# Normalising the softmax on GpSimd one step further down the pipeline, and silu then gelu back to back on ScalarE

## The reference

```python
x = x + tanh(g_xattn) * attention(layernorm(x), ctx, itok)   # 16 heads, latent keys and values of width 64
x = x + tanh(g_ffn)   * ffn(layernorm(x))

# attention, per head: (scores are scaled; keys outside itok-8 .. itok are masked)
scores = (q_nope @ k_nope.T + rope(q_rope) @ rope(k_rope).T) * scale
attn   = softmax(where(good, scores, -1e30))
out    = (attn @ v) @ W_o

# ffn
h = silu(bitlinear158(x, w1, b1)); h = gelu(h, approximate=False); h = layer_norm(h, g, b)
return bitlinear158(h, w2, b2)
# bitlinear158(x, w, b): xq = round(x_rms * 127/amax) / (127/amax), ternary w, einsum + b
```

## Time and profile before

| | us |
|---|---|
| median of 3 runs | 267.58 (265.24 to 270.92) |
| the profiled execution | 266.58 |
| its span, first to last instruction | 264.8 |
| up to the first softmax maximum | 43.3 |
| tiles 0 to 2, to the mark of tile 2 | 55.7 |
| from there to the mark of tile 3 | 24.1 |
| the next four tiles, mark to mark | 23.8, 23.6, 23.6, 23.3 |
| from the mark of tile 7 to the end | 47.3 |

### The profile page before, as it was taken

How to read it: one execution, slowest core, us unless ns; L and a number is a source line. 1 busy time by engine, 2 the same in 40 slices (tenths; PEclk the granted TensorE clock), 3 DMA queues, 4 the chain that set the end, 5 groups by cost and what they waited for, 6 DMA issues and landing times.

```text
span 264.8 us, 5090 instructions
## 1 busy us (share of the span) xinstructions
PE 221.6 (84%) x1637; PEld 196.9 (74%) x1644; DVE 204.2 (77%) x510; ACT 147.4 (56%) x327; POOL 85.4 (32%) x126
## 2 busy tenths in 40 slices
PE   1899992989999999799999999999999977934354
PEld 1677981879899899698898898889898966712232
DVE  2694543468969667998999999899989987989871
ACT  2366603634644539554945775495567549859131
POOL 1325441223423323434344333445333340111210
PEclk9999996899999999999999999999999999985557
DMA  6999990000000000000000000000000000000000
GB/s 210 265 217 236 348 375 17 0 0 2 0 2 0 0 4 1 2 1 0 4 20 0 0 19 1 0 0 20 0 0 0 22 0 0 20 0 2 21 20 28
DMA packets 11349, 12.31 MB, mean 46 GB/s; under 512 B 3936, under 2 KB 10336, under 8 KB 11104
## 3 DMA queue, kind: packets, MB, share of 16 engines
q1 hardware_dynamic: 10432, 11.44, 15.3%
q10 hardware_dynamic: 896, 0.61, 0.8%
HBM read 11.00 MB, written 1.05 MB: 45 GB/s over the span
## 4 chain that ended last, share of the span: by engine, by line
DVE 32%; PE 24%; issue 15%; SPq 11%; POOL 6%; DMA 4%; ACT 3%; DVEq 2%; POOLq 0%
SPq L344 11%; DVE qcat L1107 4%; PE bank_ff L891 4%; DMA b_bc<-in_L_ffn_b 4%; POOL h_small L430 3%; PE bank_pair L771 3%; PE bank_lat L872 3%; DVE h L1197 3%; DVE neg_max L1256 3%; DVE turned L1111 3%; PE bank_ff L920 2%; DVE z L1176 2%; DVE h L1166 2%; PE bank_prob L861 2%; DVE lat L1267 2%
## 5 line engine op out<-in xcount | busy, mean ns | idle before, releaser
L404 POOL TENSOR_TENSOR qcat<-qcat,turned 64x256 f32<-64x256 f32 x32 | 23.0, 720 | 106.5 <-DVE turned L1111 106.5
L623 ACT ACTIVATE prob_room<-bank_score,neg_max 128x128 f32<-128x128 f32 x128 | 36.5, 371 | 28.8 <-DVE neg_max L1256 28.5
L872 PE MATMUL bank_lat<-kvc,probT_room 128*128 128x65 f32 (+1 forms) x256 | 32.8, 271 | 3.5 <-ACT probT_room L613 3.5
L849 PEld LDWEIGHTS bank_score<-kcat,qcat 128*128 128x128 f32 x256 | 33.6, 192 | 2.3
L872 PEld LDWEIGHTS bank_lat<-kvc,probT_room 128*128 128x128 f32 x256 | 31.3, 193 | 5.0 <-ACT probT_room L613 5.0
L771 PE MATMUL bank_pair<-qcT,wcat 96*128 96x128 f32 (+1 forms) x256 | 34.8, 280 | 0.0
L849 PE MATMUL bank_score<-kcat,qcat 128*128 128x128 f32 (+1 forms) x256 | 33.7, 275 | 0.0
L1107 DVE TENSOR_TENSOR qcat<-bank_pair,cst 128x512 f32<-128x512 f32 x32 | 21.9, 684 | 14.0 <-PE bank_swap L774 14.0
L771 PEld LDWEIGHTS bank_pair<-qcT,wcat 96*128 96x128 f32 x256 | 32.0, 196 | 0.2 <-DVE wcat L1096 0.2
L604 ACT COPY latT<-bank_lat 128x256 f32<-128x256 f32 x32 | 11.8, 369 | 35.3 <-PE bank_lat L879 35.3
L406 POOL TENSOR_TENSOR qcat<-qcat,turned 64x256 f32<-64x256 f32 x32 | 30.5, 953 | 2.5
(11 more groups left out here) (162 smaller groups left out, 420.8 us busy)
## 6 DMA issues: line engine op xcount, KB each, us to landing
wo<-in_L_xattn_W_o SPq DMA_DIRECT2D x1, 2048.0 KB, 19.2
w_sb<-in_L_ffn_w SPq DMA_DIRECT2D x2, 1024.0 KB, 10.2
out_x<-y SPq DMA_DIRECT2D x8, 128.0 KB, 1.7
wuq<-in_L_xattn_W_uq SPq DMA_DIRECT2D x1, 768.0 KB, 10.9
ctx_all<-in_ctx ACTq DMA_DIRECT2D x2, 256.0 KB, 5.1
x_all<-in_x SPq DMA_DIRECT2D x2, 256.0 KB, 4.8
cst<-in_consts SPq DMA_DIRECT2D x1, 512.0 KB, 7.0
x_all<-in_x SPq DMA_DIRECT2D x1, 512.0 KB, 8.1
```

What stands on the lines that cost most here:

```text
L623: last = nc.scalar.activation(prob[:, k % 2, j, 0:kts * P], src[:, j, :], ACT.Exp, bias=neg_max[:, k % 2, j:j + 1])
L849: last = nc.tensor.matmul(bank[:, j * kts * P:(j + 1) * kts * P], qcat[:, k, hh // 2, hh % 2, :], kcat[:, b, hh % 2, 0:kts * P], start=Fal ...
L872: last = nc.tensor.matmul(bank_lat[:, j * (KVC + 1):(j + 1) * (KVC + 1)], probT[:, k % 2, kt, j, :], kvc1[:, b * KT + kt, :], start=(kt == ...
```

## The change

Five things change at once.

1. The softmax sum comes from the accumulator of the exponentials (`accum_out=esum`). DVE `invert_sums` takes its reciprocal one step later, POOL multiplies the 128 x 512 exponentials by it in SBUF, and the transposes wait for that. `values` now produces the latents already turned (64 rows x 256 columns, two matmuls), so `transpose_lat` and DVE's multiply are gone. With 128 keys everything from `transpose_probs` on runs two steps behind the scores (`turn_lag`), with four buffers of exponentials, and the last quarter of `attn_out` moves to step 2 of the next tile.
2. ACT applies Silu and then Gelu in step 2; its tanh and DVE's product are gone.
3. Of the small operations of `quantise` DVE keeps two. POOL computes the lower bound (power one half, times 1e-5/127), the reciprocal root and the dequantisation factor; for x also the variance terms.
4. DVE waits for b1, b2, g and lb only where it first uses each.
5. All loops are written out.

```diff
@@ SBUF, order of steps
+        def turn_lag(kts):
+            return 2 if kts == 1 else 1
@@ POOL
+            def floor_and_root(small_of, floor_ready):
+                link(small(small_of(FLOOR), small_of(MS), pos_half, ALU.pow))
+                nc.gpsimd.tensor_scalar(small_of(FLOOR), small_of(FLOOR), 1e-5 / QMAX, 1.0, ALU.mult, ALU.mult).then_inc(floor_ready, 1)
+                link(small(small_of(RRMS), small_of(MS), neg_half, ALU.pow))
             def root_hq(c):
                 pool.wait_ge(h_sumsq, c + 1)
                 link(small(hs(MS), hs(SQ), eps1, ALU.add))
-                small(hs(RRMS), hs(MS), pow_half, ALU.pow).then_inc(h_rrms, 1)
+                floor_and_root(hs, h_floor)
+            def dequantise(small_of, layer, deq, scale_ready, count, deq_ready):
+                pool.wait_ge(scale_ready, count)
+                nc.gpsimd.tensor_scalar(deq, small_of(YMAX), small_of(RRMS), wmean[:, layer:layer + 1],
+                                        ALU.mult, ALU.mult).then_inc(deq_ready, 1)
+            def normalise(f, k, kts):
+                n = step_no(f, k)
+                pool.wait_ge(rsum_done, n + 1)
+                p = prob_of(n, kts)
+                nc.gpsimd.tensor_tensor(p, p, rsum[:, k % 2, :].unsqueeze(2).broadcast_to([P, GROUP, kts * P]),
+                                        ALU.mult).then_inc(prob_scaled, 1)
                 for k in range(STEPS):
+                    if step_no(f, k) >= 1:
+                        normalise(*behind(f, k, 1), kts)
                     if step_no(f, k) + AHEAD < N:
                         add_rope_step(*ahead(f, k))
                     feed_forward(f, k)
@@ ACT
                 for j in range(GROUP):
-                    last = nc.scalar.activation(prob[:, k % 2, j, 0:kts * P], src[:, j, :], ACT.Exp,
-                                                bias=neg_max[:, k % 2, j:j + 1])
+                    last = nc.scalar.activation(prob_of(n, kts)[:, j, :], src[:, j, :], ACT.Exp,
+                                                bias=neg_max[:, k % 2, j:j + 1], accum_out=esum[:, k % 2, j:j + 1])
-                        if k == 1 and there(f, 2):
-                            tanh(f - 2)
                         if k == 2 and there(f, 3):
                             copy_h(f - 3, 0)
                         if k == 2 and there(f, 2):
-                            gelu(f - 2)
+                            silu(f - 2)
+                            gelu(f - 2, 1.0)
@@ PE
             def transpose_probs(f, k, kts):
-                pe.wait_ge(exp_done, n + 1)
+                pe.wait_ge(prob_scaled, n + 1)
             def values(f, k, kts):
-                for j in range(GROUP):
-                    for kt in range(kts):
-                        last = nc.tensor.matmul(bank_lat[:, j * (KVC + 1):(j + 1) * (KVC + 1)], probT[:, k % 2, kt, j, :],
-                                                kvc1[:, b * KT + kt, :], start=(kt == 0), stop=(kt == kts - 1))
+                for kt in range(kts):
+                    for o in range(2):
+                        last = nc.tensor.matmul(bank_lat[o * KVC:(o + 1) * KVC, 0:2 * P].rearrange("p (j s) -> p j s", j=2),
+                                                kvc1[:, b * KT + kt, :], probT[:, k % 2, kt, o::2, :],
+                                                start=(kt == 0), stop=(kt == kts - 1))
-            def transpose_lat(f, k): ...
+                if k == 2 and there(f, 1) and lag == 2:
+                    attn_out(f - 1, range(STEPS - 1, STEPS))
@@ DVE
-                link(nc.vector.tensor_scalar(small(YMAX), small(AMAX), small(RRMS), 1e-5, ALU.mult, ALU.max))
-                nc.vector.tensor_scalar(deq, small(YMAX), 1.0 / QMAX, wmean[:, layer:layer + 1], ALU.mult, ALU.mult)
-                link(nc.vector.reciprocal(small(YINV), small(YMAX)))
-                link(nc.vector.tensor_scalar(small(QMUL), small(YINV), QMAX, small(RRMS), ALU.mult, ALU.mult))
+                dve.wait_ge(floor, count)
+                dve.wait_ge(dve_link, amax)
+                nc.vector.tensor_scalar(small(YMAX), small(AMAX), 1.0 / QMAX, small(FLOOR), ALU.mult, ALU.max).then_inc(scale, 1)
+                dve.wait_ge(scale, count)
+                link(nc.vector.reciprocal(small(QMUL), small(YMAX)))
-                    quantise_h(f - 3, lambda: silu(f - 2))
+                    quantise_h(f - 3)
-            def normalise(f, k): ...
+            def invert_sums(f, k):
+                dve.wait_ge(exp_done, n + 1)
+                nc.vector.reciprocal(rsum[:, k % 2, :], esum[:, k % 2, :]).then_inc(rsum_done, 1)
             dve.wait_ge(gates_done, 1)
-            for name in ("b1", "b2", "g", "lb"):
-                dve.wait_ge(in_sems[name], 16)
...
```

More of the change, by code:

```diff
@@ L283, in choose, with run_tiles @@
                 main(KT)
-        LEAD = 3
-        def run_tiles(eng, body, after, before=lambda f: None):
-            for f in range(LEAD):
-                before(f)
+        def run_tiles(body, after):
+            for f in range(F):
                 body(f)
-            before(None)
-            with eng.Fori(LEAD, F - 1) as f:
-                before(f)
-                body(f)
-            before(F - 1)
-            body(F - 1)
             after()
         def slot(c):
-            return 1 if known(c) and c == F - 2 else 0
+            return 1 if c == F - 2 else 0
         def last_tile(c):
-            return known(c) and c == F - 1
+            return c == F - 1
         def down_bank(c):
@@ L379, in _ @@
         def _(pool):
-            half = R // 2
+            rope = R // 2
             pool.wait_ge(consts_made, 1)
@@ L407, in add_rope @@
                 pool.wait_ge(pair_done, s + 1)
-            with pool.Fori(0, B // 2) as i:
-                for e in range(2):
-                    b = 2 * i + e
-                    add_rope(kcat[KVC:P, b, 0, :], kcat[0:R, b, 1, :], turned[KVC:P, e, :], turned[0:R, e, :], b)
+            for b in range(B):
+                add_rope(kcat[KVC:P, b, 0, :], kcat[0:R, b, 1, :], turned[KVC:P, b % 2, :], turned[0:R, b % 2, :], b)
             def add_rope_step(f, k):
@@ L608, in copy_probT @@
                 n = step_no(f, k)
-                if not (known(n) and n < 2):
+                if n >= 2:
                     act.wait_ge(lat_ready, n - 1)
@@ L836, in scores @@
                 lag = 1 if kts == 1 else 0
-                if not (known(n) and n <= lag):
+                if n > lag:
                     pe.wait_ge(exp_done, n - lag)
@@ L905, in up @@
                 pe.wait_ge(xqT_copied, c + 1)
-                if waits and not (known(c) and c < 2):
+                if waits and c >= 2:
                     pe.wait_ge(y_done, c - 1)
@@ L947, in main @@
             def main(kts):
+                lag = turn_lag(kts)
                 def body(f):
@@ L962, in body @@
                             transpose_x(f - 2)
-                        feed_forward_mid(f, k)
-                        if not known(f) or 1 <= n < N + 1:
-                            values(*behind(f, k, 1), kts)
-                        feed_forward_end(f, k)
+                        feed_forward_mid(f, k, lag)
+                        if n >= lag:
+                            values(*behind(f, k, lag), kts)
+                        feed_forward_end(f, k, lag)
                         prepare_end(f, k)
@@ L1237, in feed_forward @@
                 if k == 1 and there(f, 3):
-                    quantise_h(f - 3, lambda: silu(f - 2))
-                elif k == 1 and there(f, 2):
-                    silu(f - 2)
+                    quantise_h(f - 3)
                 if k == 2 and there(f, 1):
@@ L1314, in after @@
                     output(F - 1)
-                run_tiles(dve, body, after, before)
+                run_tiles(body, after)
             choose(dve, main)
```

257 lines of the change are left out of this document (125 added, 132 removed).

## The result

| | before | after |
|---|---|---|
| median of the comparison (20 runs each) | 269.98 | 265.71 |
| lowest to highest | 265.24 to 271.35 | 263.02 to 269.85 |
| the profiled execution, its span | 266.58, 264.8 | 263.1, 261.3 |
| first softmax maximum | 43.32 | 37.39 |
| from there to the mark of tile 2 | 55.74 | 47.91 |

The ratio is 0.989 [0.985, 0.994]: 1.1% faster, which is less than the 2% that count as a change. The forecast was 262.2 us and -2.0%.

The account below looks back on a forecast made before the run. PE and DVE were taken as nearly full, PE alone binding early tiles. From the profiled 266.58 us, -5.2 - 1.9 - 7.9 - 1.7 + 1.2 + 6.0 + 2.3 + 2.8 = -4.4 gave 262.2, range 251 to 271.

Parts of the forecast that it names:

- start, wait: Start: without DVE's four weight waits the first softmax maximum comes at 38.15 instead of 43.32, -5.2 us.
- start clock and tiles 0 to 2: Start and PE-bound first tiles: no clock fall, -1.9 us; no latent transposes and shorter `values`, -7.9 us.
- mark 2 to 3: Move from tile 2 to 3: no `down` and a smaller pause, 22.4 instead of 24.1, -1.7 us.
- four full tiles at full clock: Full tiles: period 23.95 against 23.6, +0.3 us per tile, +1.2 over four.
- falls of the clock in them: Full tiles: PE's pause drops the clock in three of four, 2.0 us lost each, +6.
- tail: From mark 7: later exponentials, multiply and lag less quantisation savings, +2.3 us; clock fall after PE's pause, +2.8 (0 to 5).
- the pause: Full tile, step 3: PE idles 3.4 us ahead of `values`, waiting for ACT's copy of the turned exponentials.
- The slow multiply: Rival, POOL in full tiles: big multiply near 3.2 us, delaying the root twice; 281 us, slower; chance 0.07.
- The early gain: Rival, start and tiles 0 to 2: gain eaten, PE's cut not the bound, weight loads hold start; 268 us; chance 0.13.
- the 84 that was asked: Sign: mark of tile 2 near 84; above 88 would show the forecast wrong.
- The clock did hold: Rival, full tiles: PE's pause does not cost the clock; 253.5 to 256.5 us; chance 0.27.
- Better still: Rival, full tiles: not held by ACT, DVE's 4 us a tile show; period 22, 248 us; chance 0.08.

Follow-up runs that it names:

- 5: Changed kernel, last step of tile 7: DVE's last reciprocal moved ahead of output and moments, 267.6 us; also POOL's last multiply ahead of tile 5's root, 265.6 us.
- 7: Changed kernel with ACT tanh, DVE product and both last-step queues reordered (248.1 us), plus quantise's small operations back on DVE except reciprocal roots: 249.1 us.
- before_waits: Kernel before, with only DVE's waits moved: b1 to its first use, b2, g and lb to the end of tile 2; 261.0 us, ratio 0.986.
- 1: Changed kernel with ACT computing tanh in step 1 and DVE the silu product again, Gelu alone in step 2: 251.5 us, ratio 0.935.
- 2: Changed kernel with tanh and DVE product restored, plus one unread single-column Silu (a table load) ahead of Gelu in step 2: 265.5 us.
- 9: Kernel before with DVE's waits moved, loops written out, and Silu then Gelu on ACT in step 2: 275.5 us, ratio 1.033.

## Why the prediction was wrong, and what of it held

| step | forecast | profiled run |
|---|---|---|
| start, wait | -5.2 | -5.9 |
| start clock and tiles 0 to 2 | -9.8 | -7.8 |
| mark 2 to 3 | -1.7 | -1.4 |
| four full tiles at full clock | +1.2 | +1.1 |
| falls of the clock in them | +6.0 | +1.6 |
| tail | +5.1 | +8.9 |
| sum | -4.4 | -3.5 |

That the sums lie only 0.9 apart is luck: the tail is 3.8 and the first tiles 2.0 dearer than forecast, the falls 4.4 and the start 0.7 cheaper. The forecast gave 0.55 to a gain of more than 2%, and the gain is 1.1% by the ratio.

- *The step that failed is the tail.* It says that "the big multiply and the lag add 0.4, three quantisations give back 0.4 each". This took the last multiply nearly for free, and no line asked what stands ahead of the reciprocal on DVE and of the multiply on POOL. The kernel before had these two lines:

```profile
224.89 1.14 ACT L623 ACTIVATE prob_room<-bank_score,neg_max 128x128 f32<-128x128 f32 x4
232.56 0.48 DVE L1212 SCALAR_TENSOR_TENSOR x_all<-bank_ff,tgate,x_all 128x256 f32<-128x256 f32 x1 [0.31 <-PE bank_ff L891]
```

  Up to the end of these exponentials the changed tail is 3.2 longer (S + 11.7, before S + 8.5), exactly as forecast. From there to the last residual it is 5.7 longer, where 0.4 and 2.8 for the clock were forecast; 2.6 of it are the two queues (5), and the remaining 3.1 agree with the 3.2 of multiply and clock, but no run splits them. From the last residual to the end it takes 32.3, before 32.2, so the 1.2 that the quantisations were to give back did not come. DVE has less to do there but waits for POOL's bound, 0.81 in the first of them (231.80), where it did not wait before, and 1.12 in the second (245.70), where it waited 0.83. Undoing change 3 lengthened the tail by 0.4 in all (7). The 2.6 and the 1.2 are the 3.8 that the forecast lacks.
- *Clock.* The place and the cause were right: PE idle behind ACT's copy. Three falls were forecast at 2.0 each, and the profiled run had one, of 1.6. Their number is not fixed: the profiled runs of 5, whose full tiles are the same, had three, for 5.8 us. The other runs of the changed kernel left no trace; by their mean clocks many had more falls than the profiled one.
- *The time itself.* The forecast was added to the profiled execution of the kernel before, 266.58, as if every run were like it. In the comparison that kernel's median is 269.98, 3.4 above that execution, and the changed kernel's median is 2.6 above its own. So the measured 265.71 lies 3.5 above the forecast though the sums differ by 0.9.
- *Start.* The -5.9 is partly luck too. The changed kernel and the eleven made from it share their code up to the first softmax maximum, and it came at 37.39 in this run, the earliest, and at 37.84 to 40.09 in the others.
- *Tiles 0 to 2* came 2.0 short. In before_waits the clock at the start gave 1.1 and not 1.9. And `values` takes 0.58 from its start to that of the next piece and not 0.47, measured as the 0.84 of the earlier trace rows was, which is 0.11 in each of twelve steps:

```profile
60.52 0.58 PE bank_lat L906 x4
```

- *The full tile* was right leg by leg: the pause is 3.12 for 3.4, the multiply 1.04 for 1.3, DVE's wait 1.84 for 2, the period 23.86 for 23.95. The reason is shown (1, 2, 9): it is ACT's queue ahead of the copy. Gelu starts at 187.70, right where its load ends (186.41 + 1.28). The Trainium skill, ScalarE: Activation LUTs, section What ACT_TABLE_LOAD costs, puts a drain of about 1.38 us there, and the trace does not agree.
- *Change 5* was not in the sum. It gives 0.5 us a tile, four times. Against 23.13, changes 1 to 3 cost 0.7 a tile in the steady state, and not the 0.2 that stands between 23.86 and 23.63.
- *The rivals.* The slow multiply fell at once. The early gain was not eaten: the mark of tile 2 is at 85.30, near the 84 that was asked. The clock did hold in three of four full tiles, but not in all. "Better still" had its period, 22, exactly, but wanted it from DVE's saving; it comes when that saving is handed back (1).
- *The parts*, by profiled executions: from 266.58 changes 4 and 5 take 8.0 (258.54), about 6 for the waits and 2 for the unrolling. Changes 1 and 3 take another 7.0 (251.55): they are 12 faster up to the mark of tile 7 and 5.4 slower in the tail. Change 2 adds 11.6 (263.10). Change 1 was never run by itself.

## What to carry to other kernels

Before work is moved off a busy engine, look at what queues behind it where it goes: 1.3 us of DVE's time cost 2.4 us on ACT, straight ahead of the copy for which PE waits. All of it together cost 1.8 us a tile, and a bare table load at the same place came back one for one (1.5 for 1.5). When a handover is late at the end of a program, follow every queue between producer and consumer before editing one. A bundle of changes is priced part by part: here two small ones alone give more than the whole, and one eats what the pipeline gives. And when the time of a kernel varies from run to run, a forecast needs to say to which run it is added.
